# Top-p attention network on one core: second step's logits and exponentials moved up, its maxima begun later in the search

## The reference, cut to what matters

```
for n in range(2):                       # the two steps; N = 3327 rows, d = 128
    q = Xa @ W1.T @ W2.T ;  k = Xa @ W3.T
    probs = softmax(q @ k.T)             # N x N
    # per row: keep the largest entries until their sum reaches 0.9, drop the rest
    A = probs * keep ;  A = A / A.sum(-1)
    Xf = R @ Xf                          # R = (adj + I) / row sums
    Xa = A @ Xa
    Z = Z + Xf @ U1[n].T + Xa @ U2[n].T
out = layernorm(x + layernorm(x + Z) * g + b)
```

## Time and profile before

| | us |
|---|---|
| three runs | 1434.26, 1433.92, 1429.52 (median 1433.92) |
| the profiled execution | 1431.37 |
| its span | 1429.3 |
| busy PE / DVE / ACT / POOL | 1228.1 / 1281.5 / 930.7 / 340.5 |

### The profile page before, as it was taken

One profiled execution on the slowest core, in us unless ns is written; L12 is line 12 of the kernel. 1 busy time (PEld: TensorE's weight loads), 2 busy tenths in 40 slices (PEclk: granted clock), 3 DMA queues, 4 the chain that ended last, 5 costly groups with the idle time before them and its releaser, 6 DMA issues.

```text
span 1429.3 us, 29789 instructions
## 1 busy us (share of the span) xinstructions
PE 1228.1 (86%) x9162; PEld 1036.5 (73%) x9162; DVE 1281.5 (90%) x7010; ACT 930.7 (65%) x2026; POOL 340.5 (24%) x584
## 2 busy tenths in 40 slices
PE   7999999999997979897989796919895885929896
PEld 3677777777785968887888786818784775828796
DVE  5998989998976888899989989999998999999995
ACT  5888887788757565756575555636764746646764
POOL 0112322232201331312141220202332222212242
PEclk9999999999998989998999898969998897969998
DMA  5000000000021541412132132211312041211421
GB/s 205 2 1 2 2 2 2 2 2 2 2 97 49 193 145 38 156 49 97 55 139 96 50 103 91 97 48 49 145 50 96 2 145 49 94 52 50 145 49 49
DMA packets 16599, 96.49 MB, mean 68 GB/s; under 512 B 1251, under 2 KB 8930, under 8 KB 9730
## 3 DMA queue, kind: packets, MB, share of 16 engines
q1 hardware_dynamic: 16384, 94.14, 18.7%
HBM read 92.43 MB, written 1.70 MB: 66 GB/s over the span
## 4 chain that ended last, share of the span: by engine, by line
PE 44%; DVE 37%; ACT 11%; issue 5%; POOL 1%; DVEq 1%; DMA 0%; SPq 0%; ACTq 0%; POOLq 0%
PE bank L623 24%; DVE cand L841 13%; PE bank L602 11%; DVE junkC L898 8%; PE bank L554 5%; ACT E L696 4%; DVE E L1241 2%; ACT blkT L721 2%; ACT cand L691 2%; DVE sub L1064 2%; DVE E L1261 1%; PE bank L638 1%; DVE junkS L898 1%; DVE slots L963 1%; ACT S L696 1%
## 5 line engine op out<-in xcount | busy, mean ns | idle before, releaser
L721 ACT ACTIVATE blkT<-bank 128x512 f32<-128x512 f32 (+1 forms) x728 | 406.4, 565 | 284.7 <-PE bank L602 280.7
L841 DVE MAX8 cand<-E 128x8 f32<-128x32 f32 (+1 forms) x2992 | 404.2, 192 | 41.8 <-ACT E L674 26.4
L623 PEld LDWEIGHTS bank<-X,blkT 128*128 128x128 f32 x2704 | 329.1, 191 | 104.1 <-ACT blkT L721 71.8
L623 PE MATMUL bank<-X,blkT 128*128 128x129 f32 (+1 forms) x2704 | 375.9, 281 | 10.3 <-ACT blkT L721 9.1
L602 PE MATMUL bank<-ident,S 128*128 128x128 f32 x1560 | 242.0, 275 | 17.4 <-POOL S L451 15.6
L602 PE MATMUL bank<-ident,E 128*128 128x128 f32 x1144 | 183.0, 285 | 81.0 <-DVE E L1261 81.0
L898 DVE SCALAR_TENSOR_TENSOR junkC<-cand,st 128x128 f32<-128x128 f32 (+2 forms) x390 | 236.0, 613 | 2.0
L623 PE MATMUL bank<-YF,blkT 128*128 128x128 f32 x1352 | 192.7, 287 | 36.1 <-ACT blkT L721 36.1
L623 PEld LDWEIGHTS bank<-YF,blkT 128*128 128x128 f32 x1352 | 171.6, 199 | 68.7 <-ACT blkT L721 57.6
L554 PE MATMUL bank<-kT,Q 64*128 64x512 f32 (+1 forms) x728 | 197.0, 613 | 8.7 <-ACT E L674 8.4
L602 PEld LDWEIGHTS bank<-ident,E 128*128 128x128 f32 x1144 | 143.7, 148 | 83.3 <-DVE E L1261 82.1
(11 more groups left out here) (226 smaller groups left out, 1336.6 us busy)
## 6 DMA issues: line engine op xcount, KB each, us to landing
S<-in_adj_dram SPq DMA_DIRECT2D x50, 1663.5 KB, 6.8
S<-in_adj_dram SPq DMA_DIRECT2D x2, 1455.6 KB, 8.5
X<-in_x_dram SPq DMA_DIRECT2D x6, 256.0 KB, 5.4
out_dram<-H SPq DMA_DIRECT2D x1, 1408.0 KB
S<-in_adj_dram SPq DMA_DIRECT2D x2, 194.9 KB, 9.7
u_in<-in_L_gnn_U_dram SPq DMA_DIRECT2D x4, 64.0 KB, 9.6
out_dram<-H SPq DMA_DIRECT2D x1, 128.0 KB
w_in<-in_L_gnn_W_dram SPq DMA_DIRECT2D x2, 32.0 KB, 2.1
```

Of the source, the lines that this page charges most:

```text
L623: m = pe.matmul(bank[int(u.acc)][:, 0:width], blkT[:, slot, b * P:(b + 1) * P], rhs[:, j, 0:width], start=(j == 0), stop=(j == NT - 1))
L721: act.activation(blkT[:, slot, 0:w], BLK[early][slot][:, 0:w], ACT.Copy).then_inc(blk_done, 1)
L841: v.max(cand[:, par, xx, 8 * r:8 * r + 8], E[where_e[self.s, self.p]][:, xx, r * w:min((r + 1) * w, N)]).then_inc(s_max, 1)
```

## The change

The logits of pair p+2 stand two steps earlier in every body of the second step (14 to 20 for 16 to 22). The exponentials of bodies of four stand two steps earlier (34 to 39 for 36 to 41); those of bodies of three stay at step 36. In the search, `fill` is no longer set to 3 in front of the fine part, but to 4 behind the first of its three short trials.

```diff
@@ -64,6 +64,8 @@
     UT_AT = 4
     STEP_R = [4, 3] * 6 + [0]
+
+    EXPS_AHEAD = 2
@@ -162,10 +164,10 @@
         if p + 2 < NPAIR:
             for c in range(NCH):
-                b.emit[2 * NCH + 2 + c] = (1, p + 2, c)
+                b.emit[2 * NCH + c] = (1, p + 2, c)
 
             for k in range(6):
-                b.exps.setdefault(5 * NCH + 1 + (k if STEP_R[p] > 3 else 0), []).append((1, p + 2, k))
+                b.exps.setdefault(5 * NCH + 1 + (k - EXPS_AHEAD if STEP_R[p] > 3 else 0), []).append((1, p + 2, k))
@@ -968,7 +970,6 @@
                     link(v.tensor_reduce(two(TOTAL), slots[:, :, :], AX.X, ALU.add))
-                    link.fill = 3
                     link.post(v.tensor_tensor(two(FLOOR), two(FLOOR), two(FLOOR2), ALU.max))
                     link(v.tensor_tensor(two(TOTAL), two(TOTAL), two(LOWW), ALU.subtract))
                     link(v.tensor_tensor(two(BUDGET), two(BUDGET), two(TOTAL), ALU.add))
@@ -979,7 +980,10 @@
-                    trials(link, c, scratch, fact[C:C + F], 1.0)
+                    trials(link, c, scratch, fact[C:C + 1], fact[C + 1])
+
+                    link.fill = 4
+                    trials(link, c, scratch, fact[C + 1:C + F], 1.0)
```

## The result

The changed kernel takes 1447.78 us (median of 6 runs, 1445.56 to 1450.12), the kernel before 1431.72 (6 runs, 1428.89 to 1434.26): 16.1 us more, ratio 1.0113, 95% interval [1.0097, 1.0129]. I had forecast +6.6 us, that is 1440.5, with a range from 1427 to 1448. The profiled execution took 1445.56 us.

A forecast was written before the change was run, and what follows sets the result against it. PE and ACT bound step two to 802.6 us, DVE to 1282.0, then PE and ACT. Terms 3.6 + 3.5 - 2.1 + 1.6 = +6.6 us gave a median of 1440.5 us, range 1427 to 1448.

The forecast's parts named there:

- rival C: Bodies 0, 2 and 4: the exponentials' last piece holds PE up by 1.68 us each; 1445.5 us, chance 0.17.
- Bare links: Search, pairs 5 to 10: five links without fill lose 0.6 us an iteration, +3.6 us.
- rival A: Search: waits of small links cost nothing, so bare links cost 0; sum +0.5 us, 1434.4 us, chance 0.15.
- Second flag: Pairs 5, 6, 8, 9, 10: no maxima left to cover the second flag, +0.7 us each, +3.5 us.
- Logits' wait: Start of pair 6: DVE's 2.10 us wait for the first logits goes, -2.1 us.
- rival D: Pair 6: later maxima take most of the 2.10 us wait anyway; same sum, chance within the forecast's 0.45.
- second stretch: From the search of pair 5 to body 10: DVE bounds, almost without waits; forecast 5.0 us longer.
- It costs 0 ... POOL's own queue is not moved: Logits' move: the third R unit's load is issued 2.5 us later, POOL's queue stays; cost 0 unless a load exceeds 11 us.
- Exponentials in bodies 0 and 2: PE and ACT there: 2.7 us won at the start, 2.6 lost at the end, taken as 0.
- In bodies 4 to 8: ACT's wait for `max_ready` comes two steps earlier; in bodies 4 and 8 PE has room, so 0.
- Body 10: Exponentials start 1.0 us earlier, not 2.7, and the drain's 2.6 us remain: +1.6 us.
- Rival B: First stretch: DVE bounds it too, so its waits of 12.8 us are won; 1430.1 us, chance 0.12 alone.

The follow-up runs named there:

- e3: Kernel before with only the maxima begun later, behind the first fine trial, 4 a link; ratio 1.0024 to the kernel before.
- e4: Kernel before with only the maxima begun behind the first fine trial, 3 a link so some remain for the second flag; ratio 1.0021.
- e1: Kernel before with only the logits two steps up, in all bodies; ratio 1.0046 to the kernel before.
- g1: Kernel before with only the logits two steps up, in bodies 4 to 10 alone (pairs 6 to 12); ratio 0.9992.
- e2: Kernel before with only the exponentials of bodies of four two steps up; ratio 1.0056 to the kernel before.
- g3: Kernel before with only the exponentials two steps up in bodies 0, 2, 4, 6 and 8, not in body 10; ratio 1.0050.
- h2: Kernel before with all logits two steps up and VectorE's masks of pairs 0 to 3 reading one tensor, not two (output differs); ratio 1.0000.
- g4: Kernel before with only the exponentials two steps up in bodies 0 and 2 alone; ratio 1.0004 to the kernel before.
- h1: Kernel before with exponentials two steps up in bodies 0 to 8 and each R unit load from body 4 on issued as two halves; ratio 1.0004.
- h4: Kernel before with logits two steps up in bodies 4 to 10 and R unit loads from body 4 on in two halves; 1430.52 us, ratio 0.9988.

## Why the prediction was right or wrong, point by point

The direction was right, and 1447.78 lies in the range, by 0.2 us. That is luck: the upper end was the price of rival C "with a little more", and C is not what happened. The change cost 9.5 us more than forecast, and the main causes that the experiments found, the hold of GpSimd and the late fetches, stand in no term of my sum. By my own measure of 7.2 us the changed kernel is plainly slower, to which I gave 0.34.

- **Bare links, +3.6: right.** 0.61 us an iteration, 0.6 forecast, and the pitch of L974 to L975 is 0.19 as in the earlier trace rows. The rule of the Trainium skill ("VectorE: DVE Perf Modes", "The DRAIN you can't avoid") that would make it 0, rival A, does not hold here: e3 and e4 are slower than before with intervals above 1.
- **Second flag, +3.5: the path right, the size about half.** Flag to `settle` takes 2.33 to 2.35 us, pair 0's 2.33, and `close` stands in front. From the first bare link to `settle`, less 0.6 for the bare links and with the wait of 2.10 added back in pair 5, it was +1.1, +0.4, +0.3, +0.1 and +0.1 us in pairs 5, 6, 8, 9 and 10, 2.0 in all. Pairs 4, 7 and 11, with one flag, scatter from -0.3 to +0.4 by the same measure.
- **Logits' wait, -2.1: right, but not by the logits alone.** It is gone in the changed kernel, in e1 and in g1. It is gone in e3 too, where only the maxima begin later:
```profile
826.68 0.47 DVE L841 MAX8 cand<-E 128x8 f32<-128x32 f32 x4
```
There ScalarE stored the first logits from 825.74 on, and VectorE's first maxima came with no wait. So rival D (the later maxima take the wait anyway) holds; as it said, the sum is the same.
- **The second stretch came to +5.3 for +5.0, in part by luck.** The last stall there, 1.86 us at 1044.66, no term had: an 8 KB instruction packet went at 1042.72, while the load issued at 1037.05 ran out. In this execution it stands for what the flags fell short of (3.7 + 2.0 - 2.1 + 1.9 = 5.5); in e2 and g3 the same cause costs 4 and 6 us.
- **The step that failed first: "It costs 0 ... POOL's own queue is not moved".** GpSimd's queue was not moved, but VectorE's masks were moved over it. I counted an earlier mask in bodies 0 and 2 as a wait traded for a later wait, and didn't ask what the mask does to others while it runs. In bodies 0 and 2 the save of one R unit and the diagonal of the next lie where the masks of pairs 1 and 3 now fall, and PE has no room there: 2.4 us of idle in the changed kernel and a clock of 0.83 behind it, 4.9 in e1. The profile of before shows the hold: GpSimd's diagonal at 521.54 takes 3.59 us where others take 0.46. The Trainium skill, "SBUF — State Buffer", "Who interferes with whom", says that a VectorE instruction with two SBUF inputs contends with a GpSimd instruction that reads SBUF, and one with at most one, outside the two-port modes, doesn't. The traces agree: 37 of 38 held in the changed kernel, and none of 11 under h2's mask.
- **Exponentials in bodies 0 and 2, 0: right** (g4, 1.0004), and rival C wrong there. Its sign did come, a search of pair 5 behind 804 (807.66), but from the hold and a later start. **In bodies 4 to 8, 0: wrong.** "this falls where PE has room" is true for PE, but these bodies issue loads, and a body that ends at another time puts them over VectorE's fetches: g3 less g4 is 0.46%, 6.6 us, and h1 gives it back.
- **Body 10, +1.6: the size isn't settled.** ScalarE began at 57.1 (57.4 forecast). Alone it costs 0.9 us by the ratio, interval -0.4 to 2.1. But the end of the profiled execution is 4.0 us longer, and the table tells why: executions with a clock loss of 3.6 to 5.2 us take 147.1 to 148.5 behind body 10, those with 7.7 to 8.2 take 150.3 to 151.3. My sum had no term for the clock. The six of the second kind have a granted clock of 0.50 over the whole first 5 us of body 10 and a low stretch more, of 3.4 us, that starts 56 to 57 us into it; the other eight have neither (0.51 to 0.69 in these 5 us). What sends an execution to the one or the other is open: all three with body 10's exponentials moved are of the second kind, but so are g1, h1 and h2, where they are not.
- **Rival B** falls: the search of pair 5 starts no earlier in any run by more than 1.8 us, counted from search 0.

What stays open: the 1.5 us ahead of step two's first search. That search starts at 447.9 in g1 and at 450.8 in h4, though only later code differs. And the changed kernel with both causes taken away was not tried, so it isn't shown that they and the maxima are its whole loss. In the profiled execution the causes with a place are 1.5 ahead of the change, 3.5 around the hold, 5.3 in which links, flags and one fetch lie, and 4.0 with the clock.

## What to carry to other kernels

When an edit moves one engine's long operation in time, lay it over the other engines' timelines at its new place: over GpSimd if it reads two tensors from SBUF, and over VectorE's branches if it is a load. In this case a forecast that only counts waits and queue positions came near where one engine bounded the stretch (+5.0 for +5.3, one chance fetch included) and failed where two were nearly level. A moved step worth under 3 us was smaller here than what such meetings took or gave.

## What the runs showed of the hardware that I had not expected

- A GpSimd operation on SBUF of 0.46 us takes up to 3.9 us if it starts under a VectorE operation of 3.69 us with two tensors; under one with a single tensor and the same 3.68 us it takes 0.46.
- An 8 KB instruction fetch that meets a 1663.5 KB load is mostly served only as the load, of 5 to 6 us, runs out (21 of 29 in its last 1.2 us). VectorE goes on about 1.9 us behind the packet, with idle gaps of 1.5 to 6.0 us at ends of branches. When a fetch was asked for, no trace shows; that it waits is inferred from this and from h1. Two half loads, one behind the other, took 4.7 of 5.2 us of such gaps away in the tails.
- The granted clock after a stall differs between executions of nearly the same work: 0.50 for the first 5 us of body 10 and then 0.77 to 0.78 at 70 to 85 us in six of them, 0.51 to 0.69 and then 0.82 to 0.94 in eight, which is about 3 us of span.
